# A top-k attention stage: VectorE fetches the count of doubtful rows from PSUM itself

## The reference

```python
HEADS, DHEAD, TOPK = 8, 32, 64
q, k, v = (heads(_conv1x1(x, W, b)) for W, b in ((Wq, bq), (Wk, bk), (Wv, bv)))
scores = jnp.einsum('bhnd,bhmd->bhnm', q, k) * DHEAD ** (-0.5)
kth = jax.lax.top_k(scores, TOPK)[0][..., -1:]
masked = jnp.where(scores >= kth, scores, jnp.finfo(scores.dtype).min)
attn = jax.nn.softmax(masked, axis=-1)
o = jnp.einsum('bhnm,bhmd->bhnd', attn, v)
o = _conv1x1(o, Wo, bo) + x
h1 = jax.nn.relu(_batchnorm(_conv1x1(o, W1, b1), g1, be1))
x = _batchnorm(_conv1x1(h1, W2, b2), g2, be2) + o
# second layer: normalised x, full softmax attention without top-k, output projection, + x
```

## Time and profile before

| | |
|---|---|
| median of 3 runs | 5868.32 us (5866.23 to 5868.85) |
| the profiled execution | 5872.33 us |
| its span, first to last instruction | 5870.20 us |
| mean granted clock of TensorE | 0.82 |
| TensorE, VectorE, ScalarE busy | 74% each |
| GpSimd busy | 26% |

### The profile page before, as it was taken

How to read it: one execution, slowest core, us unless ns; L and a number is a source line. 1 busy time by engine, 2 the same in 40 slices (tenths; PEclk the granted TensorE clock), 3 DMA queues, 4 the chain that set the end, 5 groups by cost and what they waited for, 6 DMA issues and landing times. The chain is left out here.

```text
span 5870.2 us, 115806 instructions
## 1 busy us (share of the span) xinstructions
PE 4366.5 (74%) x32459; PEld 2810.7 (48%) x32459; DVE 4365.0 (74%) x25530; ACT 4327.3 (74%) x6804; POOL 1500.0 (26%) x362
## 2 busy tenths in 40 slices
PE   7565566666676366666666666998999999999998
PEld 4343344444444244444444444435556556655655
DVE  4888888888888888888888887313577777777775
ACT  2787799888898588988899889342567666666765
POOL 0343344443444244434444444001000000000000
PEclk8676677777777677777777777998999999999999
DMA  5000000000000000000000000102210101001012
GB/s 188 6 16 14 6 15 16 7 15 15 7 16 15 4 15 10 12 15 14 8 15 15 7 15 14 41 7 101 93 29 21 29 20 30 20 21 28 22 28 82
DMA packets 79588, 154.72 MB, mean 26 GB/s; under 512 B 8120, under 2 KB 49464, under 8 KB 73528
## 3 DMA queue, kind: packets, MB, share of 16 engines
q1 hardware_dynamic: 78904, 146.72, 8.8%
HBM read 99.50 MB, written 47.19 MB: 25 GB/s over the span
## 5 line engine op out<-in xcount | busy, mean ns | idle before, releaser
L565 DVE MAX8 a_top<-a_scores 128x8 f32<-128x36 f32 x18432 | 1829.3, 180 | 254.9 <-ACT a_scores L446 254.5
L547 POOL TENSOR_TENSOR a_probs<-a_scores,a_probs 128x2304 f32<-128x2304 f32 x288 | 1458.1, 5084 | 2081.7 <-ACT a_probs L462 2081.7
L373 PE MATMUL a_ps_t<-ident,a_probs 128*128 128x128 f32 x5184 | 976.8, 326 | 1045.4 <-ACT a_probs_t L457 685.8
L373 PEld LDWEIGHTS a_ps_t<-ident,a_probs 128*128 128x128 f32 x5184 | 675.4, 164 | 1333.9 <-ACT a_probs_t L457 865.0
L1108 PE MATMUL b_ps_t<-ident,b_soft 128*128 128x128 f32 x5184 | 795.2, 286 | 97.2 <-ACT b_soft_t L1181 68.7
L462 ACT ACTIVATE a_probs<-a_scores,a_steep_kth 128x2304 f32<-128x2304 f32 x290 | 641.1, 2211 | 294.1 <-DVE a_minus_max L671 294.1
L1193 DVE TENSOR_SCALAR_CACHE_REDUCE b_soft<-b_ps_s 128x2304 f32<-128x2304 f32 x290 | 741.6, 2557 | 89.0 <-PE b_ps_s L1095 70.1
L1181 ACT ACTIVATE b_soft_t<-b_ps_t 128x512 f32<-128x512 f32 (+1 forms) x864 | 438.0, 525 | 488.4 <-PE b_ps_t L1108 487.7
L1108 PEld LDWEIGHTS b_ps_t<-ident,b_soft 128*128 128x128 f32 x5184 | 558.6, 142 | 450.2 <-issue 304.1
L457 ACT ACTIVATE a_probs_t<-a_ps_t 128x512 f32<-128x512 f32 (+1 forms) x1440 | 725.7, 546 | 18.2 <-PE a_ps_t L373 6.8
L363 PE MATMUL a_ps_s<-a_k_stack,a_q_ring 128*128 128x512 f32 (+1 forms) x1465 | 652.2, 605 | 13.5 <-ACT a_scores L446 8.9
(11 more groups left out here) (126 smaller groups left out, 4420.7 us busy)
## 6 DMA issues: line engine op xcount, KB each, us to landing
a_k_stack<-k_parts SPq DMA_DIRECT2D x72, 288.0 KB, 5.9
b_k_stack<-k_parts SPq DMA_DIRECT2D x72, 288.0 KB, 6.0
a_q_ring<-q_parts SPq DMA_DIRECT2D x294, 64.0 KB
b_q_ring<-q_parts SPq DMA_DIRECT2D x294, 64.0 KB
k_parts<-p_high SPq DMA_DIRECT2D x36, 256.0 KB, 2.1
k_parts<-p_rest SPq DMA_DIRECT2D x36, 256.0 KB, 2.1
q_parts<-p_high SPq DMA_DIRECT2D x36, 256.0 KB, 2.0
q_parts<-p_rest SPq DMA_DIRECT2D x36, 256.0 KB, 2.0
```

What stands on the lines that cost most here:

```text
L373: last = pe.transpose(ps_t[(NTG * s + g) % 2][:, P * m:P * m + P], probs[s % 2][:, P * (m0 + m):P * (m0 + m) + P], cst["ident"][:, :])
L547: pool.tensor_tensor(probs[u][:, :], scores_all[:, 2 * (p % 2) + u, :], probs[u][:, :], ALU.subtract).then_inc(masked_ready, 1)
L565: last = dve.max(top8[s // 2 % 2][:, s % 2, c, :], scores_all[:, s % 4, CHUNK * c:CHUNK * c + CHUNK])
```

## The change

`keep_any` and its two kinds of calls go from ScalarE. In `hand_on`, VectorE waits for `doubt_counted`, copies the three counts from PSUM into `any_doubt` itself, raises `any_ready`, and drains before it loads the register. Since ScalarE's copy no longer stands in front of the `keep_turned` for which the odd tile's first `weigh` waits, TensorE gets an explicit wait for `any_ready` there, ahead of writing into `ps_o`. At the end of the stage VectorE waits for the last count and raises `any_ready` once more, for the last pair.

```diff
-            def weigh(s, g, tile):
+            def weigh(s, g, tile, pair):
                 pe.wait_ge(turned_kept, tile * NTG + g + 1)
+                if s % 2 == 1 and g == 0:
+                    pe.wait_ge(any_ready, pair + 2)
...
-            def keep_any(pair):
-                act.wait_ge(doubt_counted, pair + 1)
-                act.activation(any_doubt[:, :].bitcast(F32), ps_o[0:1, FLAG_COL:FLAG_COL + 3],
-                               ACT.Copy).then_inc(any_ready, 1)
...
-            keep_any(0)
...
                     keep_scores(s + 5, tile + 5)
-                    keep_any(pair + 1)
                     keep_turned(s + 1, 0, tile + 1)
...
                 dve.sem_clear(dve_order)
                 at["n"] = 0
-                wait_alone(dve, any_ready, pair + 1)
+                dve.wait_ge(doubt_counted, pair + 1)
+                dve.tensor_copy(any_doubt[:, :].bitcast(F32), ps_o[0:1, FLAG_COL:FLAG_COL + 3]).then_inc(any_ready, 1)
+                dve.drain()
                 doubtful = dve.value_load(any_doubt[0:1, 2:3], min_val=0, max_val=0x44000000)
...
             dve.wait_ge(any_ready, ALL_PAIRS)
             dve.sem_inc(doubt_ready, 1)
+            dve.wait_ge(doubt_counted, ALL_PAIRS + 1)
+            dve.sem_inc(any_ready, 1)
```

More of the change, by code:

```diff
@@ L419, in _ @@
                     pe.wait_ge(parts_ready, pair + 1)
-                    weigh(s, 0, tile)
+                    weigh(s, 0, tile, pair)
                     turn(s, 2, tile)
                     turn(s, 3, tile)
-                    weigh(s, 1, tile)
+                    weigh(s, 1, tile, pair)
                     turn(s, 4, tile)
-                    weigh(s, 2, tile)
-                    weigh(s, 3, tile)
+                    weigh(s, 2, tile, pair)
+                    weigh(s, 3, tile, pair)
                     pe.wait_ge(probs_ready, tile + 2)
                     turn(s + 1, 0, tile + 1)
-                    weigh(s, 4, tile)
+                    weigh(s, 4, tile, pair)
                     count_doubts(pair + 1)
@@ L432, in _ @@
                     turn(s + 1, 2, tile + 1)
-                    weigh(s + 1, 0, tile + 1)
+                    weigh(s + 1, 0, tile + 1, pair)
                     turn(s + 1, 3, tile + 1)
-                    weigh(s + 1, 1, tile + 1)
+                    weigh(s + 1, 1, tile + 1, pair)
                     turn(s + 1, 4, tile + 1)
                     for g in range(2, NTG):
-                        weigh(s + 1, g, tile + 1)
+                        weigh(s + 1, g, tile + 1, pair)
                     add_quadrants(pair)
```

## The result

| | before | after |
|---|---|---|
| median of 4 runs | 5867.59 us (5866.23 to 5868.85) | 5903.04 us (5898.15 to 5905.89) |
| the profiled execution, its span | 5872.33, 5870.20 us | 5898.15, 5896.4 us |

The ratio is 1.006, with a 95% interval of 1.0042 to 1.0077: the change costs 35.5 us. Within the top-k stage they tell more. From the first thresholds to the last, before took 3508.4 us and after 3540.6.

What follows compares the result with a forecast made beforehand. It took late thresholds, on a loop through ScalarE's guess, VectorE's select, MAX8 and count read, to bound the kernel. 144 x 0.11 = 15.8 us for the copy, all else 0, on 5868.3 gave 5884.1 us, range 5871 to 5908.

Steps and rivals of the forecast that it cites:

- the likeliest case: VectorE's copy is serial, overlaps the last MAX8, and some gaps move; chance 0.60, range 5876 to 5895 us.
- What bounds the kernel: Top-k stage: no engine full, order of waits decides; thresholds reach ScalarE's penalty late in all 144 pairs, 294.1 us.
- the loop that sets a pair's time: ScalarE guess, VectorE select, twelve MAX8, count read, thresholds, ScalarE penalty and its own work until the next guess; 22.64 us.
- the old gate: VectorE's register load in hand_on followed the end of ScalarE's copy, mean distance 0.14 us, not the MAX8.
- ScalarE's relief: Losing keep_any brings ScalarE to penalty(0) 0.05 us earlier, only to wait longer: gain 0; rival, 7 us faster, chance 0.05.
- TensorE's wait: Wait before the odd tile's first weigh is covered by about 0.9 us: price 0; rival that it holds TensorE, 0.03.
- The copy's term: In hand_on, VectorE's copy and drain behind twelve MAX8 start the register load 0.11 us later a pair, 15.8 us in all.
- The moved code: Shifted VectorE code may move the 0.31 us idle gaps before L670, in 44 pairs; direction unknown, so nothing added.
- the rival: Gaps behind the branch vanish, each winning 0.31 us, leaving under 11.7 us of loss; chance 0.15.
- a number of long gaps far from 44: Sign of a wrong forecast: the longer idle before L670 appearing in a pair count far from 44.
- The ScalarE total: ScalarE's summed idle in front of penalty(0) was to grow from 294 to about 317 us.
- a slow copy: Rival: VectorE's PSUM copy is slow or held, 0.20 to 0.29 us a pair, 5897 to 5910 us; chance 0.17.

Runs made afterwards that it cites:

- before_plus_one: Kernel before, with one VectorE semaphore instruction added between the wait for any_ready and the register load, nothing waiting for it: 5884.27 us, 1.0026.
- early_hand_on_only: Kernel before, ScalarE still copying, with hand_on behind 4 MAX8 instead of 12: 5872.63 us, 1.0009.
- scalar_filler: Kernel after, with an unread ScalarE copy of three constants and its wait for doubt_counted where keep_any stood: 5898.78 us, 1.0053 of before.
- tensor_wait_only: Kernel before, with only TensorE's new wait for any_ready ahead of the odd tile's first weigh: 5863.94 us, 0.9995.
- drain_only: Kernel before, with only a VectorE drain between the wait for ScalarE's copy and the register load: 5892.21 us, 1.004.
- after_minus_one: Kernel after, one VectorE instruction fewer a pair, the wait for the sums sitting on the reciprocal itself: 5892.84 us, 1.0039 of before.
- early_copy: Kernel after, with hand_on behind 4 MAX8 instead of 12: 5787.63 us, 0.9863 of before.

## Why the prediction was right, and where it was not

The forecast was 5884.1 us, in a range of 5871 to 5908, slower at 0.65. It came out slower, at 5903.04, inside the range but 18.9 us above the value given and outside the likeliest case's own 5876 to 5895.

*What bounds the kernel*: this step failed in part. A delay behind the register load is paid in full, as the forecast read from its rows. But it put `select` and the twelve MAX8 on the loop that sets a pair's time, and in the kernel before they were not on it: 0.36 us more in front of `select` cost nothing (before_plus_one), and eight MAX8 fewer won nothing (early_hand_on_only). There the loop stays on ScalarE, from the guess through its own work to its copy of the count, and reaches VectorE only at the register load. The forecast's own reading of the old gate says the same, and its sum used that reading, so the number didn't suffer here. What it missed is that the change moves the gate: behind it the load follows VectorE's order, and `select` and the MAX8 come onto the loop. In that kernel the forecast's loop holds. A copy 0.1 us later lengthened the ordinary pair by 0.11, and copies 0.39 and 0.69 us earlier shortened the pairs until ScalarE stopped waiting.

*ScalarE's relief and TensorE's wait at nothing*: right, by scalar_filler and tensor_wait_only.

*The old gate was ScalarE's copy*: right, by early_hand_on_only and by the 6.71 us from guess to load.

*The copy's term, 0.11 us a pair, 15.8 us*: right. `doubt` to load grew by 0.099 us a pair, 14.0 us in 142 pairs. Of it 6.3 us are the drain (drain_only), the other 7.7 the copy in its place. The copy took 0.129 us where 0.15 was taken, under even the lower bound of 0.14. By the rule of the Trainium skill on held instructions ("VectorE: DVE Perf Modes", section "Two Vector instructions with no wait between them") the copy at partition 0 would not be held, and the trace agrees: it starts 0.10 us behind the start of the last MAX8. The Trainium skill's 125 ns for VectorE's access to PSUM, doubled in a profiled row ("Perfetto Trace Analysis", section "Optimizing Scalar/DVE Operations"), would have made it an estimated 0.25 us; the 129 ns decide against it.

*The moved code*: this step failed. It said: "Nothing says which way, so the centre stays", and it counted gaps behind the branch alone. Behind the branch the change did win a little, as the rival had it (44 long gaps became 30, and the stretch fell by 1.4 us). But the sum had left out that such a gap can come at other lines on the loop too. In front of `select` there had been none in 144 pairs, so there they could only appear, and 29 did, for 10.3 us. They were paid because of the new gate: with the same 29 gaps, before_plus_one loses nothing by them. On ScalarE the missing instruction brought another 4.7. Moved code thus cost about 14 us, as much as the copy itself. The forecast said that a number of long gaps far from 44 would make it wrong. Behind the branch, where it counted them, 30 stand, and 29 more in a new place.

The ScalarE total shows the same. The forecast had 317 us, the trace has 327.4 in after and 319.9 in after_minus_one, where the gaps in front of `select` are gone.

The sum by the runs: 14.0 for copy and drain, 10.3 in front of `select`, -1.4 behind the branch, 4.7 on ScalarE, and 2.2, 2.1 and 1.0 in the remaining stretches (`penalty(0)` to `parts`, the rest of the seventh, and the two small ones), 32.9 us. What is not settled: the last 5.3 us, which no run isolates. TensorE's granted clock in the stage was 0.72 against 0.73, which may hold some of them. And the medians of kernels with a single part differ from the pair sums by a few us (15.8 against 13.0, 24.0 against 17.3), so the parts are known to about that. That the forecast's range held is thus partly luck: it reached 5908 for the sake of a slow copy, which didn't come, and the gaps filled that room.

Also open is why code at some places gets a gap. No row names an instruction that is fetched, but the traces hold DMA packets of a kind called instruction, with their times. The page of after counts those of one queue, nearly all of 8192 bytes:

```profile
q14 instruction: 425, 3.48, 0.2%
```

In after such a packet starts 0.55 to 1.0 us behind the start of `select` in all 29 pairs with the long gap and in 7 of the 113 without it. Behind the start of `steep_kth` it does in 23 of the 30 pairs with a long gap and in none of the 95 with a short one (the other 17 are the pairs with doubtful rows). So gap and fetch go together; no run holds the fetches fixed, and that they are the cause is argued. The Trainium skill ("Runtime: NRT & Kernel Launch", section "Instruction fetch mechanics") says that instructions are prefetched in sequence and that a taken branch out of the fetched pages stalls for a fetch. It would fit the gaps behind the branch in `hand_on`. At place 6 no branch stands directly in front of `select`, only chunks of MAX8 and semaphore instructions, and the gap is 0.35 us as well, so that rule alone doesn't cover it.

## What to carry to other kernels

When a small serial step moves from one engine to another, ask first what its place in the new engine's order is: the same copy cost 0.6% behind twelve MAX8 and won 1.4% behind four, because only on its new engine could it be moved up. Where instructions are added to or removed from a long written-out loop on the engine that is waited for, compare every stretch of the loop by the place in it, not the changed line alone, and run a kernel with one idle instruction more and one with one less before a difference under half a per cent is put down to the change's idea. Put the idle instruction where nothing waits for the code behind it: between a wait and the register load it cost 0.09 us a time by itself. Split the pairs by whether they have a gap before summing; a sum of 2.0 us hid 9.7 us more in some pairs and 7.7 less in others. And ask of a gap whether it is paid: it is free while the engine would wait for another one anyway, and a change that moves the gate can start to charge for it. Look for idle times that come in two sizes at fixed places, and count also the lines that have none yet.

## What the runs showed of the hardware

- One more semaphore instruction between VectorE's wait and its register load, for which nothing waits, cost 15.8 us of 5868, 0.26%. The load came 0.225 us behind the end of ScalarE's copy where it had come 0.132 behind.
- The gaps come in nearly one size, 0.31 to 0.36 us, mostly at fixed places of an 18-pair stretch of code, and eight instructions ahead of the loop moved them from one line to another.
- A VectorE copy of 1x3 from PSUM has a median of 129 ns in after, where the count was there 0.75 us before (709.77 + 0.24 to 710.76), and of 149 ns in early_copy, where it starts 0.04 us behind the matmuls. No run says whether the nearness is the reason. ScalarE's copy of the same has a median of 145 ns in before.
- A drain behind the MAX8 delayed the register load by 0.05 us where VectorE had no gap, and by 0.39 where it had one (guess to load 6.76 and 7.10 us, against 6.71). Behind the copy the load starts 0.1 us after the copy's end.
- TensorE's granted clock differed with the schedule of the other engines. With most of ScalarE's idle time in front of `penalty(0)` gone it was 0.76 in the same stretch where after has 0.72, as a mean over its levels of 1.2 and 2.4 GHz. A matmul record took 2093.34/17855 = 117 ns in place of 2115.31/17249 = 123. TensorE was busy for 62.5% of that stretch against 63.1%, with 3.5% more instructions. The 20 us less that ScalarE waits at line 492 for TensorE would fit that; no run holds the clock fixed, so that link is argued and not shown.
